# A graph network with two expert layers on one core: the routing stage's choices and scatters two steps closer behind the logits, its gates formed once

## What is computed

```python
rh = relu(features @ router_w1 + router_b1)                  # 128 wide
expert_logits = softmax(rh @ router_w2 + router_b2)          # 6 experts
top_w, top_i = top_k(expert_logits, 2)
routing_weights = softmax(top_w)                             # the two gates of a row
h1 = relu(features @ expert_w1[e] + expert_b1[e])
h2 = relu(h1 @ expert_w2[e] + expert_b2[e])
combined = sum(over the two chosen e, (h2 @ expert_w3[e] + expert_b3[e]) * routing_weights)
```

## The kernel before, in words

| step | VectorE | ScalarE | TensorE |
|---|---|---|---|
| 4j+12 | `shift`(j) | `bn_relu` half 0 of block j+3 | `rows` third stage of j+2 |
| 4j+13 | | `exp_logits`(j), `copy`(j+1), `bn_relu` half 1 of j+3 | `turned`(j+1), `rows` last stage of j+2 |
| 4j+14 | `x1_of`(j+2), `choose_first`(j) | | `router`(j+1), `rows` first stage of j+3 |
| 4j+15 | `f1_of`(j+2), `keep`(j+1) | | `logits`(j+1), `rows` second stage of j+3 |
| 4j+16 | `choose_second`(j) | | `rows` third stage of j+3 |
| 4j+17 | | `exp_gap`(j) | `turned`(j+2), `rows` last stage of j+3 |
| 4j+18 | `x1_of`(j+3) | | `places`(j), `router`(j+2) |
| 4j+19 | `place_rows`(j) | | |

## Time and profile before

### The profile page before, as it was taken

The page is one execution under the profiler, slowest core; times in us unless marked ns, Lnnn a source line. Parts: engine busy times, 40 slices in busy tenths (PEclk is TensorE's granted clock), DMA queues, the critical chain, the costliest instruction groups (busy, mean ns, idle before and its releaser), DMA issues. The chain is left out here.

```text
span 2970.5 us, 53210 instructions
## 1 busy us (share of the span) xinstructions
PE 2622.7 (88%) x14911; PEld 2213.3 (75%) x14911; DVE 1697.2 (57%) x5391; ACT 1444.3 (49%) x4050; POOL 1791.3 (60%) x1939
## 2 busy tenths in 40 slices
PE   2999999999888899599994999999888888789998
PEld 1877777889887788488883766676677777768887
DVE  6733324788665566545553656566577767634333
ACT  4122222463222555145566978797667856422222
POOL 5777777777776255446666777777777777500000
PEclk9999999999999999699997999999999989989999
DMA  7464445777675477335554444444466655532222
GB/s 235 117 193 139 141 143 175 234 220 235 211 223 176 152 241 218 113 117 162 159 161 148 130 138 127 138 130 138 122 175 193 185 158 164 151 106 71 77 74 59
DMA packets 294758, 464.33 MB, mean 156 GB/s; under 512 B 91113, under 2 KB 227218, under 8 KB 293388
## 3 DMA queue, kind: packets, MB, share of 16 engines
q1 hardware_dynamic: 211638, 238.37, 27.1%
q0 software_dynamic: 81216, 221.98, 25.8%
q10 hardware_dynamic: 1632, 0.79, 0.1%
HBM read 349.16 MB, written 111.83 MB: 155 GB/s over the span
## 5 line engine op out<-in xcount | busy, mean ns | idle before, releaser
L2528 POOL DMA_INDIRECT g_got<-xm_d,idx x782 | 758.4, 970 | 250.7 <-issue 218.9
L883 POOL DMA_INDIRECT g_got<-xn_d,idx x702 | 681.0, 970 | 229.2 <-issue 213.3
L2167 PEld LDWEIGHTS ps<-g_hotw,g_got 128*128 128x128 f32 x3128 | 413.0, 200 | 204.5 <-DMA g_got<-xm_d,idx 163.3
L2167 PE MATMUL ps<-g_hotw,g_got 128*128 128x128 f32 (+11 forms) x3128 | 440.8, 290 | 138.5 <-DMA g_got<-xm_d,idx 133.9
L1282 PEld LDWEIGHTS ps<-g_hot,g_got 128*128 128x128 f32 x2808 | 354.6, 195 | 106.5 <-DMA g_got<-xn_d,idx 77.7
L1282 PE MATMUL ps<-g_hot,g_got 128*128 128x120 f32 (+4 forms) x2808 | 374.7, 280 | 56.8 <-DMA g_got<-xn_d,idx 55.9
L2577 ACT ACTIVATE g_hotw<-g_hot,g_wr 128x16 f32<-128x16 f32 (+8 forms) x1308 | 299.3, 309 | 34.4 <-DVE g_hot L590 34.2
L1482 POOL TENSOR_TENSOR p_ln_rs<-p_ln_pre,neg_half 125x2 f32<-125x2 f32 x50 | 35.2, 705 | 461.0 <-DVE p_ln_pre L1477 461.0
L2082 POOL DMA_INDIRECT z_d<-p_yj,p_to x108 | 127.5, 1181 | 145.5 <-DVE p_to L2115 126.2
L2999 ACT ACTIVATE p_hid<-ps,p_b 128x250 f32<-128x250 f32 x200 | 82.9, 466 | 251.7 <-PE ps L2960 251.7
L2059 PE MATMUL ps<-gin_hid,p_wj 128*128 128x256 f32 x864 | 197.4, 382 | 0.9 <-ACT gin_hid L2002 0.8
(11 more groups left out here) (387 smaller groups left out, 4856.8 us busy)
## 6 DMA issues: line engine op xcount, KB each, us to landing
h_d<-gin_hid SPq DMA_DIRECT2D x23, 1000.0 KB, 5.2
gin_hid<-h_d SPq DMA_DIRECT2D x23, 1000.0 KB
p_xr<-jobs_d SPq DMA_DIRECT2D x54, 258.0 KB, 3.0
g_got<-xm_d,idx POOLq DMA_INDIRECT x782
g_got<-xn_d,idx POOLq DMA_INDIRECT x702
p_z<-z_d SPq DMA_DIRECT2D x50, 224.0 KB
q_d<-g_qo SPq DMA_DIRECT2D x25, 250.0 KB
g_xa<-xn_d SPq DMA_DIRECT2D x50, 125.0 KB
```

The lines of the kernel that those rows point to most:

```text
L883: landed.start(e.indirect_dma_start(got[:, k % (2 * GB), :], None, xn_d[0:N, :], bass.IndirectOffsetOnAxis(ap=idx[:, HT + k:HT + k + 1], a ...
L2167: mm = e.matmul(to, rows[j][:, c * P:(c + 1) * P], hotw[:, j, c * w:4 * w].unsqueeze(1).broadcast_to([P, r, n]), start=(j == 0), stop=(j = ...
L2528: landed.start(e.indirect_dma_start(got[:, 2 * (g % GB) + j, :], None, xm_d[0:N, :], bass.IndirectOffsetOnAxis(ap=idx[:, 2 * g + j:2 * g + ...
```

## The change

The choice of the best expert moves from lag 14 to 13, that of the second from 16 to 14, the counting product on TensorE from 18 to 16, `place_rows` and the scatters from 19 to 17 (so the scatters stand at steps 21 to 120). The gap, its exponent and the three gate instructions leave the batches (16 times five instructions) and are done once on all 50 tiles: the gap behind the tails' release, the exponent behind ScalarE's padding transfers, the gates at the very end of VectorE's program.

```diff
-                    due = max(MARKS[b] + 19, due + 1)
+                    due = max(MARKS[b] + 17, due + 1)
...
-                    def exp_gap(b, lo, hi):
-                        gap.wait(e, b, "gap")
-                        gap_exp.done(e.activation(gates[:, lo:hi, 1], second[:, lo:hi], ACT.Exp), "gap")
-                    timeline(LAST_STEP, (MARKS, [(at_batch(exp_gap), 17), (at_batch(exp_logits), 13)]),
+                    timeline(LAST_STEP, (MARKS, [(at_batch(exp_logits), 13)]),
                              (POS, [(router_relu, 10), (copy, 9), (bn_relu(0), 0), (bn_relu(1), 1)]))
                     e.wait_ge(s_k, 3)
                     e.wait_ge(s_tail, 1)
                     pad_tails(e, range(1, NE0, 2))
+                    gap.wait(e, 0, "gap")
+                    gap_exp.done(e.activation(gates[:, :, 1], second[:, :], ACT.Exp), "gap")
...
-                    timeline(LAST_STEP, (MARKS, [(at_batch(places), 18)]),
+                    timeline(LAST_STEP, (MARKS, [(at_batch(places), 16)]),
...
                         pick(1, at, n, big[:, at])
-                        gap.done(e.tensor_tensor(second[:, at], best[:, 1, at], best[:, 0, at], ALU.subtract), "gap")
...
                         placed.done(e.tensor_copy(slots[0:TN, :, at], place[:, :, at]), "slots")
-                        gap_exp.wait(e, b, "gap")
-                        step(e.tensor_scalar(big[:, at], gates[:, at, 1], 1.0, None, ALU.add))
-                        step(e.reciprocal(gates[:, at, 0], big[:, at]))
-                        step(e.tensor_tensor(gates[:, at, 1], gates[:, at, 1], gates[:, at, 0], ALU.mult))
...
-                             (MARKS, [(at_batch(place_rows), 19), (at_batch(choose_second), 16),
-                                      (at_batch(choose_first), 14), (at_batch(shift), 12)]))
+                             (MARKS, [(at_batch(place_rows), 17), (at_batch(choose_second), 14),
+                                      (at_batch(choose_first), 13), (at_batch(shift), 12)]))
...
                     e.sem_inc(s_tail, 1)
+                    gap.done(e.tensor_tensor(second[:, :], best[:, 1, :], best[:, 0, :], ALU.subtract), "gap")
...
                     step(e.tensor_scalar(job_rank[:, :], ps[:, 7, NJ:2 * NJ], -1.0, 8.0, ALU.mult, ALU.add))
+                    gap_exp.wait(e, 0, "gap")
+                    step(e.tensor_scalar(big[:, :], gates[:, :, 1], 1.0, None, ALU.add))
+                    step(e.reciprocal(gates[:, :, 0], big[:, :]))
+                    step(e.tensor_tensor(gates[:, :, 1], gates[:, :, 1], gates[:, :, 0], ALU.mult))
```

## The result

The changed kernel takes 2982.38 us (median of 9 runs, 2977.38 to 2987.17) against 2972.16 us (9 runs, 2967.88 to 2976.38) of the kernel before: ratio 1.0037 [1.0029, 1.0045], so slower by 0.4%, little but clear of the noise. The profiled execution took 2984.09 us with a span of 2982.5 us.

A forecast was written before the change was run, and what follows sets the result against it. TensorE bounds the stage until 1206 us, then a chain through VectorE beside GpSimd's scatters. Steady part +16.7 and end -5.5 give +11.2 us on 2972.05; with 0.58 for the median, 2983.8 us, range 2969 to 2989.

The forecast's parts named there:

- The gates: VectorE's per-batch gate work, some 0.7 us a batch: worth 0 under TensorE's cover, and hidden at the end.
- The new wait: Steady part: `x1_of` waits for the exponent behind a reload, then TensorE at `places`; +14.7 us over nine batches of two.
- The size of the steady part: Before the stage's end: +14.7 us for nine batches of two and +2.0 for four following blocks, +16.7 us.
- single blocks: Four following blocks with reloads ahead: about two can wait, 1.7 us at most each; +2.0 us, bounds 0 and +3.4.
- Starting again: TensorE at `places` after a wait: weight load no longer runs ahead of its product, 0.1 us a time, +0.8 us.
- The clock: Rival: new waits make TensorE's granted clock fall for a block, its 9 us near doubling; 2993 us or more, chance 0.03.
- The end: Stage's end: tail 6.2 us earlier, two fewer scatters behind the last root, padding transfers end the stage; -5.5 us.
- my own lower bound: Stage's end: smallest gain, if only GpSimd's two scatters count; -2.5 us.
- The end alone: Rival: exponent early enough, `x1_of` never waits, `places` finds its mark; only -5.5 us remains, 2967 us, chance 0.12.
- Reloads run ahead: Rival: slower TensorE lets reloads land sooner, waits shrink to 8.1 us; +2.6 us, 2975 us, chance 0.16.
- VectorE was the bound: Rival: 16 batches x 0.7 us come back in the steady part, no new wait; 2956 us, chance 0.02.

The follow-up runs named there:

- the repeat: The changed kernel, unedited, measured once more beside other runs: 2989.53 us against 2975.35 for the kernel before, ratio 1.0058.
- the late release: Changed kernel with the padding transfers' release moved behind the eleventh instruction of the list of jobs, some 4 us later: 2984.58 us.
- the gates alone: Changed kernel with the old steps, only the gates still hoisted: ratio to the kernel before 0.9995, measured again 2972.71 us, 0.9998.
- the steps alone: Kernel before with the new steps, its gates still formed batch by batch: 2993.47 us against 2975.35, ratio 1.0068.
- the scatters caught up: Changed kernel with the exponent one step earlier, `places` one later, scatters' due steps advancing by 0.8 instead of 1: 2973.70 us, ratio to before 0.9995.

## Why the prediction held, and where its sizes did not

- **The gates, 0.** Right. Hoisting alone gave 0.9998 [0.9988, 1.0007], as the view with TensorE at 20.00 of 20 us said. I had not seen that `exp_gap` would hold ScalarE under the new steps. The stage was 7 to 9 us shorter without it there, mostly by the clock, and whether that is its doing is not shown.
- **The new wait.** Right in mechanism, and shown by undoing it: when the exponent is written ahead of the half of `bn_relu` that waits, the loss goes. Eight of the nine batches of two wait at `places`: 1.46, 1.00, 0.73, 1.53, 1.49, 1.32, 1.52 and 0.87 us, and in the third, which doesn't, the router had waited 2.32 us. The forecast "VectorE waits 1 to 5 us ahead of `x1_of`" holds for 11 of 12 waits; one took 5.52.
- **The size of the steady part, +16.7.** Measured +17.2 and +12.9, so the total is right, but not its make-up. The step that failed is the sum of delays: I had +14.7 for the nine batches, 0.8 of it for starting again, and +2.0 for single blocks, so 15.9 us of waiting. TensorE's idle time grew by 11.6 us in one profile (4.2 to 15.9) and 8.9 in the other. Of the 15.9 us, `places` of the nine batches takes 9.9 and the router 4.4 (0.42, 2.32, 0.92, 0.78), and the single blocks 1.2 (0.23, 0.60, 0.32).
- **Starting again, +0.8.** Too small. TensorE's timeline of the kernel before shows `places` with no wait ahead of it:

```profile
1130.31 1.89 PE L1698 MATMUL ps<-gin_w,gin_hid 128*125 128x256 f32 x8
1132.04 0.30 PE L1736 MATMUL ps<-p_taken,p_before 125*125 125x24 f32 x2
```

The product ahead ends at 1132.20, so of the 0.30 us only 0.14 stand alone. Behind a wait the same two products take 0.40 us (1135.91 in the changed kernel) and nothing runs over them. That is 0.26 us a time where I had 0.1, and some 3 us in the 11 places that wait. It is the size of the 2.5 us of busy time that the clock doesn't explain; the router, which waits in fewer places than before, gives about 1 us back.

- **The clock, chance 0.03.** I had argued from waits of 0.8 and 1.06 us that the clock would stay at 1.00, and that failed. It fell twice in the profiled execution and once in the repeat, for 3.4 us each, worth +3.4 and +1.7 us. It was not the case I had priced (a block's 9 us doubled, 2993 us), but it filled most of what the waits fell short of.
- **The end, -5.5.** Wrong in size: -2.8 in the profiled pair (38.5 us from the last `x1_of` to the next stage, against 41.3) and -0.5 in the repeat (40.8). The failed step is "It doesn't end the stage: the padding transfers do". They didn't even before: SyncE saw them land 1.7 us behind the scatters, but GpSimd came to the meeting 2.2 us later still. The tail came even a little sooner than forecast (7.47 us behind `keep`, forecast 7.9), and it did not matter, as the late release shows. What counts was my own lower bound, GpSimd's two scatters: issued 2.9 us earlier (forecast 3.0), with 11.6 to 13.9 us from there to the next stage. The forecast's own sign, that the queues hold the end if it gains less than 4 us, came true.
- **The rule of the Trainium skill.** I had set against the rows what the Trainium skill says in its page Perfetto Trace Analysis, section Optimizing Scalar/DVE Operations, that fewer and larger operations help if the engine is saturated. The trace agrees with the condition: VectorE wasn't saturated (142.49 of 217.30 us busy), and 7.1 us less of its work gave nothing.
- **Rivals.** "The end alone" fell: the exponent was never early enough. "Reloads run ahead" fell: 83.6 us of waits for them against 84.2. "VectorE was the bound" fell with the gates alone.
- **The sum.** The stage grew by 14.4 us (12.4 in the repeat) against +11.2 forecast. The timed difference is 10.2 us (14.2 in the repeat). That the forecast of 2983.8 us lies 1.4 from the median owes something to luck: the waits were 4.3 us too large (15.9 against 11.6) and the end 2.7 us too good, 5.1 of the 5.9 us of slower work were missing, and the rest of the kernel varies by as much from run to run.

## What to carry to other kernels

A step moved ahead in an in-order queue takes over what its input waits for, and hands that wait to all that now stands behind it; follow the input back through every queue to the transfer at its root before moving the consumer. At the end of a stage, look which engine comes last to the meeting, and not only which transfer lands last: an engine that waits for a transfer and then waits again was not the one to be sped up. Delaying a part tells whether it sets the end. Work taken off an engine that is 65% busy beside one at 98% was worth nothing here.

## What the runs showed of the hardware

I had not expected that waits as short as 1.5 us would be followed by a fall of TensorE's granted clock from 1.00 to 0.50. The first fall in the changed kernel (at 1051.4 us) came behind a wait of 2.32 us, and ahead of that TensorE had been busy for 4.00 of 4 us at 1.00 (1044 to 1048 us). With the steps alone all five waits of 1.54 to 1.61 us at `places` that the trace shows were followed by a fall, and TensorE's timeline of that kernel shows what it does to the stage of `rows` right behind:

```profile
1016.74 1.97 PE L1698 MATMUL ps<-gin_w,gin_hid 128*125 128x256 f32 x8
1020.25 0.40 PE L1736 MATMUL ps<-p_taken,p_before 125*125 125x24 f32 x2 [1.54 <-DVE p_sofar L1869]
...
1020.71 3.30 PE L1698 MATMUL ps<-gin_w,gin_hid 128*125 128x256 f32 x8
```

Eight products take 3.30 us instead of 1.97. In the changed kernel a wait of 1.52 us (at 1156.42) was followed by a fall, and one of 1.53 (at 1097.22) wasn't. Nor was one of 1.62 at the router with the scatters caught up (1117.69), nor one of 1.93 in the kernel before with the exponent ahead (1195.56), where one of 1.87 was (1173.18). So the length of the wait alone doesn't decide it; what does stays open. Each fall in these traces lasted 3.4 us and cost some 1.7 us beside the wait.

The end of the stage is the other one: between the landing of the last scatter that SyncE waits for and the end of GpSimd's DRAIN lay 4.1 us in ten profiles of ten, whatever landed in between.
